# A graph-attention edge loop on one core: the turn of a batch's scores after both score pairs, the row products after both pairs of sums

## The reference

```
s = x_l[src] + x_r[dst] + e_feat              # one row of 4 heads x 64 for each edge
s = leaky_relu(s, 0.2)
alpha = einsum('ehc,hc->eh', s, att)          # one score for each edge and head
amax = segment_max(alpha, dst)
ex = exp(alpha - amax[dst])
denom = segment_sum(ex, dst)
out = segment_sum(ex / denom[dst] * x_l[src], dst)
```

## Time and profile before

| what | value |
|---|---|
| median of three executions | 3392.98 us |
| span of the profiled execution, first to last instruction | 3546.6 us |
| TensorE busy in the span | 3206.4 us, 90% |
| VectorE busy | 1826.2 us, 51% |
| ScalarE busy | 1387.4 us, 39% |
| GpSimd busy | 1196.3 us, 34% |
| mean granted clock of TensorE | 0.958 |

### The profile page before, as it was taken

How to read it: one execution, slowest core, us unless ns; L and a number is a source line. 1 busy time by engine, 2 the same in 40 slices (tenths; PEclk the granted TensorE clock), 3 DMA queues, 4 the chain that set the end, 5 groups by cost and what they waited for, 6 DMA issues and landing times. The chain is left out here.

```text
span 3546.6 us, 52145 instructions
## 1 busy us (share of the span) xinstructions
PE 3206.4 (90%) x14480; PEld 2570.5 (72%) x14481; DVE 1826.2 (51%) x3687; ACT 1387.4 (39%) x4710; POOL 1196.3 (34%) x1148
## 2 busy tenths in 40 slices
PE   6789999999989998957899899889999989999989
PEld 5567776766767676636777777777777778888878
DVE  5666666766766766767353644544373424111002
ACT  2056666666666666663122212312232211222222
POOL 4556666666666666403110310120020001222200
PEclk9899999999999999978999999999999979999999
DMA  7556666665666665533010101000100042333341
GB/s 228 143 146 149 153 149 151 148 147 147 144 147 152 146 149 151 111 100 80 22 43 26 30 8 36 27 8 1 39 24 14 1 156 63 118 117 116 123 134 44
DMA packets 288629, 345.09 MB, mean 97 GB/s; under 512 B 155176, under 2 KB 213655, under 8 KB 284512
## 3 DMA queue, kind: packets, MB, share of 16 engines
q1 hardware_dynamic: 232813, 174.79, 18.5%
q0 software_dynamic: 53632, 157.89, 17.4%
q10 hardware_dynamic: 2064, 10.81, 1.0%
HBM read 298.03 MB, written 44.37 MB: 97 GB/s over the span
## 5 line engine op out<-in xcount | busy, mean ns | idle before, releaser
L1429 POOL DMA_INDIRECT a_g<-xl_d,a_ix x480 | 475.9, 991 | 297.1 <-remote 135.5
L1446 PE MATMUL a_pS<-g_xr,a_lt 128*128 x1680 | 534.8, 401 | 42.5 <-issue 19.4
L1454 PE MATMUL b_pM<-b_m,b_oh 128*112 128x281 f32 x1680 | 457.9, 413 | 23.1 <-DVE g_acc L1585 16.7
L1578 DVE SCALAR_TENSOR_TENSOR a_r<-a_pS,g_attx 128x528 f32<-128x528 f32 x420 | 288.5, 700 | 344.3 <-remote 269.8
L1541 ACT ACTIVATE b_m<-a_g,c_pcx 128x64 f32<-128x64 f32 x1856 | 455.6, 333 | 2.3 <-issue 1.9
L1429 POOL DMA_INDIRECT XS<-xl_d,a_ix x344 | 337.1, 980 | 202.8 <-issue 86.7
L1446 PEld LDWEIGHTS a_pS<-g_xr,a_lt 128*128 128x128 f32 x1680 | 310.3, 193 | 119.6 <-issue 67.2
L1454 PEld LDWEIGHTS b_pM<-b_m,b_oh 128*112 128x112 f32 x1680 | 294.2, 180 | 136.6 <-issue 39.8
L125 POOL TENSOR_TENSOR m_rstd<-m_ve,m_mhalf 125x5 f32<-125x5 f32 x41 | 48.0, 1170 | 902.8 <-DVE m_ve L111 902.8
L1541 ACT ACTIVATE b_m<-XS,c_pcx 128x64 f32<-128x64 f32 x1424 | 349.0, 333 | 1.2 <-issue 1.2
L424 PE MATMUL m_pH<-m_h,m_w 128*128 128x312 f32 (+1 forms) x1280 | 341.9, 428 | 7.7 <-DVE m_h L572 7.7
(11 more groups left out here) (399 smaller groups left out, 4412.6 us busy)
## 6 DMA issues: line engine op xcount, KB each, us to landing
a_db<-dl_d SPq DMA_DIRECT2D x212, 224.0 KB
f_w<-in_ffn_W1p SPq DMA_DIRECT2D x32, 1024.0 KB
m_w<-in_mix_W SPq DMA_DIRECT2D x8, 1024.0 KB
f_w<-in_ffn_W2p SPq DMA_DIRECT2D x8, 1024.0 KB
a_g<-xl_d,a_ix POOLq DMA_INDIRECT x480
a_lt<-eat_d SPq DMA_DIRECT2D x214, 32.0 KB
eat_d<-a_stage SPq DMA_DIRECT2D x15, 448.0 KB
ea_d<-a_stage SPq DMA_DIRECT2D x15, 448.0 KB
```

The costliest lines, as they stand in the source:

```text
L1429: p.indirect_dma_start(out=gathered(t)[:, j, :], out_offset=None, in_=xl_d, in_offset=bass.IndirectOffsetOnAxis(ap=IX[:, t // BSTEPS, n:n ...
L1446: pe.matmul(o, lt[:, j, :], XRW[:, bass.ds(ws[h], 1), :].rearrange("p a d -> p (a d)"), start=True, stop=False)
L1454: ins = pe.matmul(pM[0:WN, h, 0:MW], OH[:, b, j, :], M[:, b, j, :], start=(j == 2 * h), stop=(j == 2 * h + 1))
L1578: v.scalar_tensor_tensor(out=R[:, 2 * h:2 * h + 2, :], in0=pS[0:TE, 2 * h:2 * h + 2, 0:GD], scalar=0.0, in1=attx[:, :].unsqueeze(1).broadc ...
```

## The change

At tau = 0 TensorE now does `scores(1)` before the transpose of `a_alpha` and `sums(1)` before the row products. VectorE now does `gate(1)` before the two scans. Nothing is added or taken away. In the other slots nothing stood between the two calls of `sums`, so their order stays, and the transpose at tau = 3 stays between the score pairs. The lines of the diff that matter:

```
 TensorE, slot
                             scores(0, ws)
 
-                        if tau == 0:
-                            wait(pe, "a_alpha", base, t)
-                            pe.transpose(pA[0:CP, 0:TE], AX_[:, par, :, :].rearrange("p h i -> p (h i)"), ident[:, :]).then_inc(s["c_turned"], 1)
-                        elif tau == 3:
+                        if tau == 3:
...
                         if scoring:
                             scores(1, ws)
-                        if tau == 1:
+                        if tau == 0:
+                            wait(pe, "a_alpha", base, t)
+                            pe.transpose(pA[0:CP, 0:TE], AX_[:, par, :, :].rearrange("p h i -> p (h i)"), ident[:, :]).then_inc(s["c_turned"], 1)
+                        elif tau == 1:
...
                             sums(0)
+                            sums(1)
 
                         if tau == 0:
                             pe.wait_ge(s["c_scan"], n)
...
-
-                        if summing:
-                            sums(1)
 VectorE, slot
                             gate(0)
-                        if tau == 0:
-                            v.wait_ge(s["c_turned"], n)
-                            v.wait_ge(s[f"c_breaks{par}"], 96 * i + (0 if odd else 96))
-                            v.tensor_tensor_scan(FB[:, 0, :], BR[:, par, 0, :], scores, LOW, ALU.add, ALU.max)
-                            v.tensor_tensor_scan(FB[:, 1, ::-1], BR[:, par, 1, ::-1], scores[:, ::-1], LOW, ALU.add, ALU.max).then_inc(s["c_scan"], 1)
-                        elif tau == 2:
+                        if tau == 2:
...
                         if scoring:
                             gate(1)
+                        if tau == 0:
+                            v.wait_ge(s["c_turned"], n)
+                            v.wait_ge(s[f"c_breaks{par}"], 96 * i + (0 if odd else 96))
+                            v.tensor_tensor_scan(FB[:, 0, :], BR[:, par, 0, :], scores, LOW, ALU.add, ALU.max)
+                            v.tensor_tensor_scan(FB[:, 1, ::-1], BR[:, par, 1, ::-1], scores[:, ::-1], LOW, ALU.add, ALU.max).then_inc(s["c_scan"], 1)
```

## The result

The changed kernel takes 3395.44 us (median of 20 executions, 3388.72 to 3401.28), the kernel before in the same comparison 3390.09 us (20 executions). The ratio is 1.0018 with a 95% interval of 1.0012 to 1.0025: the medians differ by 5.35 us, and by the interval the change costs 4 to 8.5 us. The time lies inside the predicted range and within the 0.2% that counted as no change, but the interval excludes "no change": the forecast of a sum of zero was wrong. In a later job two executions (5511.41 us of the kernel before, 4198.24 us of the last experiment, at granted clocks of 0.56 and 0.74) fell into a slow state of the chip; they are in the medians and counts given here and in no ratio.

A forecast was written before the change was run, and what follows sets the result against it. The prediction took TensorE to bound the edge loop. With VectorE on time its three terms summed as 0 + 0 + 0 = 0; the forecast was 3392 us, 1 us off the median for surviving transpose pauses, range 3364 to 3416 us.

The forecast's parts named there:

- no change: Whole kernel: signals on time, or gains and losses that cancel; 3392 us, own range 3385 to 3400, chance 0.47.
- What bounds the kernel: Edge loop: TensorE is the bound, busy 1155.7 of 1250 us; its 94.3 us idle is all a new order can win, besides low-clock time.
- Which world the timed runs are in: Loop: timed runs, 153.6 us shorter than the profiled span, lack the late signals; VectorE is on time, so the sum is 0.
- The sign that the prediction named: Changed kernel's profile: transpose wait for `a_alpha` below 10 us from 36.7, row products waiting more than 6.2 us.
- The transpose behind `scores(1)`: TensorE, once a batch: four matmuls, 1.8 us, cover the wait for `a_alpha`; 0 with signals on time, 17 us saved otherwise.
- The row products behind `sums(1)`: TensorE: the second pair of sums costs the same 1.0 us either side; work between transpose and row products falls from 2.93 to 2.2 us.
- `gate(1)` ahead of the scans: VectorE: scans end at T + 1.6, row products come at T + 2.2; 0.6 us of slack, costing nothing if on time.
- What counts as no change: Measurement limit: 0.2% of the time, 6.8 us, is about what a measurement of this kernel tells from no change.
- The slower one: Row products wait for the later chain of gate and scans once lateness exceeds 0.6 us; 3422 or 3417 us, chance 0.26.
- The faster one: Stalls before the transpose are in timed runs too; 17 us of stall and 12 us of clock come off, 3364 us, chance 0.27.

The follow-up runs named there:

- the last experiment: The changed kernel with VectorE's two scans moved behind the one-hot rows as well, 0.54 us later: 3405.1 us, ratio 1.0054 to the kernel before.

## Why the prediction was wrong, by its own steps

*What bounds the kernel.* The reading was right for the trace and, for the timed runs, the right half of it was chosen: TensorE bounds the loop, the late signals are not in these runs, and the transpose waits once, 0.6 us. In the changed and the unchanged kernel TensorE idles less than 7 us in 1150.

*Which world the timed runs are in.* The conclusion held, and its argument too: 148 of the 159 us lay in the loop, where 136 had been reckoned. A reason given for it fell. NOTIFIC — the notification-queue block, section 7.1 of the Trainium skill, which says that the path that records events can hold up an engine when its internal queues fill, was read as placing the lateness in the profiled execution alone. Profiled spans of 3387.0 and 3387.2 us without it, and 34 executions above 3564 us on one chip, speak against profiling as the cause. The rule that the prediction took from the Trainium skill, Perfetto Trace Analysis, section Tensor Engine Instruction, that the signal goes out only after PSUM has acknowledged the write, does not account for it either, if it makes every execution late: in the changed kernel's trace a gate starts within 0.05 us of the modelled end of its matmul (633.52 + 0.61 = 634.13, gate at 634.16). The sign that the prediction named, row products that wait more than 6.2 us, did not appear in the changed kernel's profile, which has no late signals; it appeared on the chip that has them.

*The transpose behind `scores(1)`.* Its gain was put at 0 for on-time signals. There was 0.6 us of waiting to win in the kernel before, so it is 0 to within that; no run has this part alone.

*The row products behind `sums(1)`.* Right: nothing, by the kernel that has this part alone.

*`gate(1)` ahead of the scans.* This is the step that failed: "So 0.6 us of slack remain [...] If VectorE is on time, the wait costs nothing, hidden by the sums." The times in it were right to a tenth (scans end T + 1.54, row products at T + 2.10, 0.5 us of slack). But it took the first matmul behind the wait for the only thing that waits. TensorE's sequencer stands at the same wait, and the next slot's window load and set-up, 1.15 us, come after it. They have to be done by T + 2.84; the load starts at T + 1.72 or T + 1.80, so they are 0.03 to 0.11 us late, and the score pair starts 0.09 to 0.15 us late. That is the 0.12 us lost per turn. Loading early or scanning earlier gives it back; scanning 0.54 us later costs 0.54 us per turn (41.79 against 41.25), all of it.

*Not seen at all:* the first turn, where `summing` is still false and the row products have no cover: 1.5 us by the traces.

*What counts as no change.* The 0.2% that the prediction took for the limit of a measurement was too wide: with 20 executions each the interval is 0.07% to either side, and so a loss of 0.18% is told from none.

*The rivals.* The slower one named the right chain and the wrong deciding point: time is lost from a lateness of about 0 on, not of 0.6 us. Its size, 24 to 29 us, belongs to a chip with late signals; there similar orders lose 30 to 46 us. The faster one has nothing for it in any run, though the changed kernel itself was not run on such a chip. That the time fell near the forecast 3392 us is no proof of the sum: two terms of it were missing, and both are small.

## What to carry to other kernels

When work is moved behind a semaphore wait, two things wait: the instruction, and everything that the engine's sequencer has yet to issue, register loads and address arithmetic included. Count the set-up of the next block (here 1.15 us) from the moment the wait clears, against the work already queued at the array. Look as well at the first pass through a loop, where the work that covers a wait may not exist yet. And before a stall in one trace is costed, see that the span agrees with the timed median: here 153.6 us too much meant a trace from another condition, and of the 36.7 us of stalls in it the matching trace has 0.6. In the matching traces the span is 1.7 us below the time of its execution.

## What the runs showed of the hardware

- The kernel before had medians of 3387.3, 3388.1 and 3390.1 us in three jobs and 3571.6 us in a fourth, on another chip, where TensorE's signals reach the other engines up to 6 us after the modelled end of the work that they report, while its next matmuls already run. The cause of the late signals is open; no run here could take it away. The chip of the first profile is not on record. Whether the changed kernel is faster or slower than the kernel before on such a chip was not run; four related orders were 0.9 to 1.3% slower.
- The sequencer began the register load 0.17 to 0.33 us after the end of the scans in every steady turn, whether the scans ended at T + 1.13, 1.55 or 2.08. In half of the turns the wait stands on a register operation of its own; in the other half it stands on a weight load, and the register work behind that did not run before the wait was fulfilled either. Whether the wait itself or the instructions piled up behind it held the sequencer was not tested.
- With signals on time most distances between turns agree to 0.01 us within each kind of turn, so a loss of 0.1 us per turn can be read from one trace, where timed runs need twenty. The sum over the loop can't be read so: from the first transpose to the last it is 1192 us in the changed kernel's trace and 1194 in that of the kernel before, because of the irregular turns.
